# A two-layer transformer kernel: in its latent attention the first bank's softmax division moves to ScalarE, its reciprocal ahead of the later maxima, and unread products start without a signal

## What is computed

```python
x = x + 0.5 * ffn0(layernorm(x))     # a dense layer with routed low-rank terms
x = x + attn0(layernorm(x))          # 16 heads of 16
x = x + 0.5 * ffn0(layernorm(x))
x = x + 0.5 * experts(layernorm(x))  # 32 experts, 4 a row, silu(g) * u
x = x + attn1(layernorm(x))          # latent attention, below
x = x + 0.5 * experts(layernorm(x))

# attn1: 16 heads, 4 batches of 512 rows
scores = einsum('bqhd,bkhd->bhqk', q, k) * scale
mask = triu(full((seq_len, seq_len), -inf), k=1)
probs = softmax(scores + mask, axis=-1)
out = einsum('bhqk,bkhd->bqhd', probs, v) @ wo
```

## Time and profile before

| | |
|---|---|
| median of 3 runs | 1463.39 us (1462.01 to 1467.23) |
| the profiled execution, whole | 1460.13 us |
| its span in the profile | 1458.3 us |
| busy in the span | TensorE 87%, VectorE 65%, ScalarE 46%, GpSimd 34% |
| stages in the span, us | first layer 0 to 507, experts m1 to 672, latent attention to 1230 (its heads 717 to 1213), experts m2 to 1458 |

### The profile page before, as it was taken

One profiled execution on the slowest core, in us unless ns is written; L12 is line 12 of the kernel. 1 busy time (PEld: TensorE's weight loads), 2 busy tenths in 40 slices (PEclk: granted clock), 3 DMA queues, 4 the chain that ended last, 5 costly groups with the idle time before them and its releaser, 6 DMA issues.

```text
span 1458.3 us, 22406 instructions
## 1 busy us (share of the span) xinstructions
PE 1262.3 (87%) x6657; PEld 824.8 (57%) x6658; DVE 952.2 (65%) x2794; ACT 670.3 (46%) x1700; POOL 491.1 (34%) x493
## 2 busy tenths in 40 slices
PE   6879888898888399998879898889889997799997
PEld 4554243343325388887646455556546655678886
DVE  6796758777778422224698979887897794133334
ACT  2205655556573055553345444553554453255550
POOL 3054040053123645552211211351153143455550
PEclk8989999999999699999999999999999999799999
DMA  8537443065313266544011100020000102355647
GB/s 287 104 36 122 182 87 44 1 120 185 137 37 149 98 230 202 193 154 170 15 44 30 29 1 1 12 105 1 8 33 18 59 33 94 127 189 183 205 138 303
DMA packets 79120, 151.89 MB, mean 104 GB/s; under 512 B 11677, under 2 KB 60254, under 8 KB 75422
## 3 DMA queue, kind: packets, MB, share of 16 engines
q1 hardware_dynamic: 63310, 108.59, 25.8%
q0 software_dynamic: 15264, 41.70, 8.0%
q10 hardware_dynamic: 432, 0.17, 0.0%
HBM read 85.29 MB, written 64.75 MB: 103 GB/s over the span
## 4 chain that ended last, share of the span: by engine, by line
PE 54%; DVE 27%; ACT 6%; issue 6%; POOL 3%; DMA 3%; SPq 0%; DVEq 0%; ACTq 0%; POOLq 0%
PE m_psG L1276 12%; PE m_psY L1292 6%; DVE a_t L1733 5%; DVE a_mx L924 4%; PE a_psA L1490 3%; DVE a_nb L1741 3%; PE a_psO L482 3%; POOL rows_dram L167 3%; PE m_psX L1267 3%; PE a_psU L1469 3%; ACT a_pr L1600 2%; PE a_psU L457 2%; PE a_psU L1478 2%; PE a_psO L1513 2%; DVE a_q L1729 2%
## 5 line engine op out<-in xcount | busy, mean ns | idle before, releaser
L167 POOL DMA_INDIRECT outs_dram<-m_ys,dest x190 | 181.9, 958 | 156.0 <-ACT m_ys L1194 150.8
L1600 ACT ACTIVATE a_pr<-a_psA,a_nb 128x512 f32<-128x512 f32 (+3 forms) x256 | 132.7, 525 | 216.0 <-DVE a_nb L1741 216.0
L1214 DVE TENSOR_TENSOR m_hm<-m_psG,m_sg 128x128 f32<-128x128 f32 x190 | 55.5, 292 | 252.9 <-ACT m_sg L1188 251.8
L924 DVE TENSOR_REDUCE a_mx<-a_psU 128x1 f32<-128x512 f32 x256 | 163.4, 684 | 63.8 <-PE a_psU L457 62.8
L1276 PE MATMUL m_psG<-arena,m_xgT 128*128 x760 | 200.4, 386 | 3.8 <-ACT m_xgT L1182 3.2
L1657 POOL TENSOR_TENSOR a_q<-a_q,a_t 64x512 f32<-64x512 f32 x64 | 80.9, 1263 | 347.4 <-DVEq L1736 325.8
L167 POOL DMA_INDIRECT rows_dram<-a_xd,slot x112 | 114.7, 1024 | 157.2 <-DVE a_xd L147 72.3
L610 ACT ACTIVATE a_P<-a_psS 128x512 f32<-128x512 f32 x256 | 142.6, 597 | 50.4 <-PE a_psS L468 48.2
L1276 PEld LDWEIGHTS m_psG<-arena,m_xgT 128*128 128x128 f32 x760 | 129.8, 191 | 20.5 <-issue 9.1
L1741 DVE TENSOR_REDUCE a_nb<-a_psA 128x1 f32<-128x512 f32 (+3 forms) x256 | 113.3, 485 | 34.3 <-PE a_psA L1492 25.0
L457 PE MATMUL a_psU<-arena 96*128 96x512 bf16 x256 | 101.6, 397 | 27.0 <-DVE a_mx L924 25.5
(11 more groups left out here) (299 smaller groups left out, 2310.3 us busy)
## 6 DMA issues: line engine op xcount, KB each, us to landing
m_xg<-rows_dram SPq DMA_DIRECT2D x46, 512.0 KB, 4.2
arena<-in_mo_w SPq DMA_DIRECT2D x9, 2048.0 KB, 9.3
arena<-part_dram SPq DMA_DIRECT2D x96, 128.0 KB, 5.6
arena<-outs_dram SPq DMA_DIRECT2D x20, 512.0 KB, 3.8
rows_dram<-a_P SPq DMA_DIRECT2D x6, 1024.0 KB, 14.6
part_dram<-a_part SPq DMA_DIRECT2D x16, 384.0 KB, 5.1
rows_dram<-arena SPq DMA_DIRECT2D x6, 1024.0 KB, 13.2
arena<-outs_dram SPq DMA_DIRECT2D x6, 1024.0 KB, 13.4
```

The lines of the kernel that those rows point to most:

```text
L167: pool.indirect_dma_start(out=rows_dram, out_offset=bass.IndirectOffsetOnAxis(ap=slot[:, c:c + 1], axis=0), in_=row, in_offset=None).then_ ...
L924: dve.tensor_reduce(mx[g % 2][:, 4 * kt + qt:4 * kt + qt + 1], psU[n % 2][:, :], AX, ALU.max).then_inc(u_free, 1)
L1600: ins = act.activation(pr[S % 2][:, AT[t]:AT[t] + (t + 1) * P], psA[:, AT[t]:AT[t] + (t + 1) * P], ACT.Exp, bias=nb[S % 2][:, t:t + 1], sc ...
```

## The change

1. ScalarE multiplies bank 0 (tile 3, 512 columns) by its reciprocal, in an activation with a per-row scale, between the exponentials of bank 0 and those of bank 1. It waits for the new semaphore `first_rec` and signals `first_quotient`, for which TensorE's turn now waits at bank 0.
2. VectorE takes the reciprocal of bank 0 right behind `queries(S + 2)`, ahead of the maxima of banks 1 and 2, and doesn't wait for its end. It no longer multiplies bank 0.
3. The semaphore `stored` is gone from both expert stages. The first run of unread products waits for the weights alone, and is 50 products in m1 (8 before) and 60 in m2 (22 before).

```diff
@@ moe_stage, TensorE
             pe.wait_ge(weights_in[0], weights_in[1])
-            pe.wait_ge(stored, 1)
-            stay_warm(pe, psY[1], ident, 8 if latent is not None else 22)
+            stay_warm(pe, psY[1], ident, 50 if latent is not None else 60)
@@ latent_stage, TensorE, turn
                 for k, ts in enumerate(BANKS):
-                    pe.wait_ge(quotient, NBK * h + k + 1)
+                    if k == 0:
+                        pe.wait_ge(first_quotient, h + 1)
+                    else:
+                        pe.wait_ge(quotient, (NBK - 1) * h + k)
@@ latent_stage, ScalarE
                     for k, ts in enumerate(BANKS):
+                        if k == 1:
+                            act.wait_ge(first_rec, S + 1)
+                            t = BANKS[0][0]
+                            pt = pr[S % 2][:, AT[t]:AT[t] + (t + 1) * P]
+                            act.activation(pt, pt, ACT.Copy, scale=rec[S % 2][:, t:t + 1]).then_inc(first_quotient, 1)
                         act.wait_ge(nb_ready, NBK * S + k + 1)
@@ latent_stage, GpSimd (and the same in first_layer)
             store(B - 1, 0, TPB * TOPK)
-            pool.sem_inc(stored, 1)
@@ latent_stage, VectorE, divide
                 step = max(hi - lo - 1, 1)
+                if k == 0:
+                    dve.reciprocal(rec[s % 2][:, lo:hi], sums[s % 2][:, lo:hi]).then_inc(first_rec, 1)
+                    return
                 link(dve.reciprocal(rec[s % 2][:, lo:hi:step], sums[s % 2][:, lo:hi:step]))
@@ latent_stage, VectorE, the loop over heads
                 maxima(S, 0)
                 if S + 2 < HEADS:
                     queries(S + 2)
+                divide(S, 0)
                 for k in range(1, NBK):
                     maxima(S, k)
-                for k in range(NBK):
+                for k in range(1, NBK):
                     divide(S, k)
```

More of the change, by code:

```diff
@@ L984, in rows @@
                     scatter(pool, b * TPB * TOPK + n, slot, rows_dram, row, placed[b % 2])
-                if b == B - 1 and hi == TPB * TOPK:
-                    pool.sem_inc(stored, 1)
                 if b < B - 1 or hi == TPB * TOPK:
@@ L1920, in program @@
         placed = [[sem(f"m{m}_placed{i}") for i in range(2)] for m in (1, 2)]
-        stored = [sem(f"m{m}_stored") for m in (1, 2)]
         picked = [sem(f"picked{i}") for i in range(10)]
```

22 lines of the change are left out of this document (11 added, 11 removed).

## The result

The changed kernel takes 1484.82 us (median of 4 runs, 1481.91 to 1484.95) against 1464.1 (4 runs, 1462.01 to 1467.23) for the kernel before on the same chip: ratio 1.0136, 95% interval 1.0115 to 1.0156. It is **20.7 us slower**. Forecast were 1466.4 us and no difference, with a range up to 1474. One execution of a later run (the last with wide products) took 1845.71 us at a mean granted clock of 0.65, where the others had 0.96 or 0.97; it is left out of that run's median and ratio.

The account below looks back on a forecast made before the run. VectorE's own stream was taken to set 45 of 64 heads, TensorE's scores the other 19. Terms 0 + 3.6 + 0 + 1.0 - 1.1 - 0.5 = +3.0 us on 1463.4 gave 1466.4 us, no difference, range 1458 to 1474.

Parts of the forecast that it names:

- The unread products: Runs ahead of the expert transposes: no change in m1, earlier expert start in m2; -0.5 us, ends +1.0 and -1.8.
- The reciprocal's place: Bank 0's reciprocal ahead of the maxima joins VectorE's chain: 0.08 us on 45 heads, +3.6 us, ends 0 and +9.0.
- the rival that decides for slower: Latent heads: the reciprocal costs its full 0.20 us on the chain; +8.4 us in sum, 1471.8 us; chance 0.13.
- The multiplication of bank 0 leaves VectorE: Latent heads: bank 1's exponentials last as long either way, so VectorE idles some 0.7 us a head; 0 us.
- The rival in which the relief counts in full: Latent heads: each of 45 loses 0.73 us less 0.08, 29.3 us in all; about 1433.5 us; chance 0.10.
- The 0.01 us in the earlier trace: One head before: bank 0's multiplication on VectorE and bank 1's exponentials end within 0.01 us, so removing it gains nothing.
- the 91% of the earlier trace: VectorE's busy share in the first latent batch, 117.68 of 130 us, cited for the faster rival.
- ScalarE's multiplication: Fits ScalarE's 2.05 us idle time before bank 1's exponentials, nothing to spare; 0 us, upper end +3.6 us.
- The last two heads: No queries there cover bank 0's exponentials, so the 63rd head's reciprocal delays the maxima; +1.0 us, ends 0 and +2.0.
- Less contention with GpSimd: VectorE's 512-column multiplication, slowed beside GpSimd's addition, is gone from the heads; -1.1 us, ends 0 and -2.4.
- The range: Total time 1458 to 1474 us, topped by the slower rival with part of ScalarE's overrun; faster rival left out.

Follow-up runs that it names:

- the last with wide products: Kernel before without the store signal, its unread products replaced by 13 (m1) and 20 (m2) four times as wide: 1462.05 us against 1462.69, ratio 0.9991.
- the part alone: Kernel before with only the unread products changed, 50 and 60 without the store signal: 1478.74 us, ratio 1.0106.
- The run behind the stores: Kernel before with its 5 and 7 unread products behind the landing of the expert rows raised to 47 and 45: 1483.78 us (one run).
- the wide ones: Kernel before without the store signal, 13 and 15 unread products of 128x512 (later 13 and 20): 1464.45 us, ratio 0.9987 (later 1462.05, 0.9991).
- the run with the queries late: Changed attention, old product counts, bank 0's reciprocal behind the maxima, ScalarE's multiplication last, VectorE's queries moved behind that reciprocal: 1526.77 us, ratio 1.0464.
- the attention part alone: Changed kernel with its unread products back at 8 and 22, still without the store signal: 1471.55 us against 1464.72, ratio 1.0054.
- the reciprocal moved: Kernel before with only bank 0's reciprocal ahead of the maxima of banks 1 and 2, VectorE still multiplying: 1472.2 us against 1461.91, ratio 1.0075.
- with it back: Changed attention, 8 and 22 products, bank 0's reciprocal back behind the maxima, ScalarE's multiplication behind its last exponentials: 1466.93 us, ratio 1.0033.
- the run with 60: Kernel before without the store signal, with 24 and 30 narrow unread products (48 and 60 records): 1470.43 us against 1464.11, ratio 1.0036.

## Why the prediction was wrong

**The unread products: this step failed.** It took 0.24 and 0.12 us a record from runs of 16, 44 and 14 and multiplied it to 100 and 120 records. The arithmetic of the clock was not the main fault: behind the stores, 94 records took 12.61 us. The step assumed that a record costs the same however many stand ahead of it, and no row of before had more than 44 in a piece. The 100 records in m1 were forecast at 12.8 us and took 22 (496.59 to about 518.5), since from the 26th on they came through only haltingly until GpSimd's stores had ended. -0.5 us was forecast, with +1.0 as the upper end; the part alone measured +15.5. The run behind the stores shows that the products by themselves go through, and the wide ones that the clock was to be had; what was left out was another resource, which the gaps of "issue" and the wide products point to as the supply of instructions, and what disturbs it, GpSimd's stores. None of the rivals had it either: each added the same -0.5.

**The reciprocal's place: mechanism right, size wrong.** I took 0.08 us a head from two small operations 0.07 apart and called 0.20 the upper end, with a chance of 0.13 as the rival that decides for slower. It is 0.19 or 0.20 in all 62 heads with queries. That the earlier trace rows has 0.20 too is in part luck, since there the next operation waits for the reciprocal's end and here nothing does. And 0.08 was not wrong for the operation as such: in the run with the queries late, the same reciprocal stands between maxima and queries and takes 0.06 to 0.08 us in 62 heads. The number of heads was wrong as well, the other way: 26 distances grew by this amount, not 45. I had counted only the waits for scores; in the same stretch of the earlier trace rows VectorE also waits 24 times for a query product and 9 times for a side product:

```profile
DVE x L1796 <- PE a_psU L1469: 11.4, 9, 2.2
DVE a_q L1729 <- PE a_psU L1478: 7.4, 24, 0.7
```

The rival's 1471.8 us is close to what the attention part alone measured (1471.55, an excess of 7.9 us against the rival's 8.4), but it got there with 45 x 0.20 = 9.0, where that run has 4.9 in 25 heads and 3.9 scattered over 25 others.

**The multiplication of bank 0 leaves VectorE, 0 us: right.** VectorE's idle time took its place, 0.76 us in the mean of 62 heads (0.7 forecast). The rival in which the relief counts in full fell: not one undisturbed head got shorter, with the reciprocal moved or with it back. The 0.01 us in the earlier trace rows decided it against the 91% of the earlier trace rows.

**ScalarE's multiplication, 0 us: right in place, by 0.07 us.** It takes 722 ns in the mean, and the exponentials behind it start when the maxima allow. The estimate of 706 ns by the Trainium skill, ScalarE: Activation LUTs, section on what ACT_TABLE_LOAD costs, was 16 ns too low, and the 0.9 us made from it did not appear: the later maxima made room for it.

**The last two heads, +1.0 us: right.** The 63rd distance grew by 1.11 and 1.12 us in both kernels with the ScalarE multiplication, and by 1.13 with the reciprocal alone. Rows of that head answer: the reciprocal waits 0.91 us for the exponentials.

```profile
1224.67 0.16 DVE L1753 RECIPROCAL a_rec<-a_sums 128x1 f32<-128x1 f32 x1 [0.91 <-ACT a_pr L1605]
1224.75 0.54 DVE L1745 TENSOR_REDUCE a_nb<-a_psA 128x1 f32<-128x384 f32 x1
```

**Less contention with GpSimd, -1.1 us: seen in two heads, open in sum.** In the 61st and 62nd head the multiplication had taken 1.08 and 1.31 us. Their distances went from 6.32 to 6.19 and from 6.57 to 6.07 us, with the 0.20 for the reciprocal in them, and to 6.20 and 6.07 with the attention part alone. The other heads in which it had been slow are among the scattered distances, which are larger than this term.

**The range** ended at 1474, because the only slow case that I worked out was one of the heads. The prediction's own upper end for the products was 1 us.

## What to carry to other kernels

Instructions that do nothing are not free because the engine is idle: a run of short ones needs to be supplied, and whatever stands behind it waits until the whole run is through. If such products are to keep the clock up, few wide ones did it here without gaps (20 in 18.95 us), though the time gained was too small to show; size them to end when what they bridge is there, since what is left then is paid in full. When an edit takes work from the busiest engine, look in one head's timeline for what the next step really waits for, and when it also moves one small operation onto that chain, price the move by start-to-start distances, with their spread over several places as the range: the same reciprocal cost 0.08 us in one place and 0.20 in another. And extrapolate a pace only to lengths that some row shows.

## What the runs showed of the hardware that was not expected

A long run of short TensorE instructions breaks into pieces beside GpSimd's indexed row stores. Three runs with more than 50 records beside the stores show the same form in m1: 24 to 28 records at their own pace, 11 to 14 in 7.5 to 9 us with gaps of up to 1.7 us, then the rest in a piece that starts 2.3 or 2.4 us after the last store's instruction ends (506.54 and 508.85 in the changed kernel). In m2 62 and 63 went through first in the two runs with 120, and all 60 in the run with 60. How the stores hold the instructions up is not shown. But the stores are not the whole condition. The queues' rows for 494 to 497 us of the changed kernel show an instruction transfer ahead of the gaps, beside the stores' own (packets, MB, share of the transfer engines):

```profile
q0 software_dynamic: 96, 0.26, 24.6%
q8 instruction: 1, 0.02, 2.5%
```

All five stretches of gaps begin 3.4 to 6.2 us after such a transfer, in m1 (at 495.0 us here) and in m2 (at 1263.3 here, where the gaps begin at 1266.8). The 60 records of m2 that went through beside the stores had none, from 1247.4 to 1256.1 us. And the 90 records of m2 behind the stores had one in their midst, at 1272.9 us, and no gap:

```profile
q8 instruction: 1, 0.02, 0.5%
```

So long runs of narrow products have gaps where both are there, the transfer and the stores, and not where one is missing. In the kernel before, 44 records went through beside the stores with a transfer at 1240.9, and their run was at its end 6.3 us after it. There is no transfer from 497 to 521 us, the stretch of the gaps in m1, so it isn't a late transfer that ends them, and the stores' 24.6% of the transfer engines is no full load either. No run was made to vary the place of the transfer.

A reciprocal of 0.16 us that does not have to wait, with maxima behind it, takes 0.20 us of VectorE's stream (1201.34 to 1201.54). The same pair in the 63rd head, where the reciprocal had waited 0.91 us, is 0.08 apart (1224.67 to 1224.75). The wait isn't what makes the difference: in the 45th head above the reciprocal had not waited, and the queries start 0.08 us behind it (1110.74 to 1110.82). What sets the 62 slow places apart is that the queries stand directly ahead, whose last operation reads PSUM from another partition than the maxima do; in the fast places only maxima stand there. That this is the cause wasn't tested by itself.

VectorE's multiplication of 384 columns takes 421 ns in the mean and 1165 ns where GpSimd's addition of 64x512 runs beside it in nearly every head, and undisturbed heads take 6.13 to 6.16 us there; the one head without the addition takes 5.21.
